# Nine groups instead of eight, and a row selection that spans all 128 rows

## The reference

```
x = x + 0.5 * fp4_ffn(layernorm(x))          # feed-forward, operands rounded to FP4 in blocks of 16
x = x + mamba(layernorm(x))                  # two layers, 256 channels, state of 16
x = x + 0.5 * fp4_ffn(layernorm(x))          # same weights as the first
x = x + 0.5 * experts(layernorm(x))          # 8 experts 128 -> 512 -> 128, gated by a thresholded sigmoid
x = x + attention(layernorm(layernorm(x)))   # 16 heads of 8, causal, relative bias
x = x + 0.5 * experts(layernorm(x))          # same weights as before
```

```
h_n[t] = exp(delta[t] * A_n) * h_n[t-1] + delta[t] * u[t] * B_n[t]
y[t]   = sum over n of h_n[t] * C_n[t]
```

## Time and profile before

| | |
|---|---|
| median of the runs shown | 2872.73 us |
| profiled execution, its own time | 2876.84 us |
| its span, first to last instruction | 2875.1 us |
| mean granted TensorE clock | 0.953 |
| instructions | 41563 |
| VectorE busy | 1946.4 us (68%) |
| ScalarE busy | 1606.0 us (56%) |
| GpSimd busy | 1371.3 us (48%) |

### The profile page before, as it was taken

One profiled execution on the slowest core, in us unless ns is written; L12 is line 12 of the kernel. 1 busy time (PEld: TensorE's weight loads), 2 busy tenths in 40 slices (PEclk: granted clock), 3 DMA queues, 4 the chain that ended last, 5 costly groups with the idle time before them and its releaser, 6 DMA issues.

```text
span 2875.1 us, 41563 instructions
## 1 busy us (share of the span) xinstructions
PE 2733.4 (95%) x14913; PEld 1895.2 (66%) x14913; DVE 1946.4 (68%) x3753; ACT 1606.0 (56%) x3405; POOL 1371.3 (48%) x1226
## 2 busy tenths in 40 slices
PE   7999999999999989999799899999999999999888
PEld 7777875786577655666366566656575666678675
DVE  5868887697868687676867886687858666432320
ACT  2433436435664556656486556756675676465654
POOL 2448475563737365454716474274636635311111
PEclk9999999999999989799799999999999999999899
DMA  4223122131213021211202121121202112000000
GB/s 147 67 67 104 55 64 74 45 92 42 79 40 96 23 73 39 70 49 49 77 20 78 37 76 31 49 70 31 75 19 86 36 52 67 1 4 1 1 5 4
DMA packets 88573, 150.60 MB, mean 52 GB/s; under 512 B 10565, under 2 KB 21485, under 8 KB 88110
## 3 DMA queue, kind: packets, MB, share of 16 engines
q1 hardware_dynamic: 88366, 147.94, 16.4%
HBM read 145.26 MB, written 2.65 MB: 51 GB/s over the span
## 4 chain that ended last, share of the span: by engine, by line
PE 83%; ACT 7%; DVE 5%; POOL 3%; issue 2%; DMA 0%; POOLq 0%; SPq 0%; ACTq 0%; DVEq 0%
PE c_bank L912 16%; PE c_bank L920 16%; PE c_bank L1338 13%; PE a_bank L758 8%; PE a_bank L748 5%; PE b_bank L1072 3%; PE b_bank L1061 3%; PE a_bank L727 2%; PE b_bank L1085 2%; PE b_bank L1084 2%; PE b_bank L582 1%; PE b_bank L563 1%; PE b_bank L565 1%; PE b_bank L1083 1%; PE a_bank L764 1%
## 5 line engine op out<-in xcount | busy, mean ns | idle before, releaser
L829 POOL TENSOR_TENSOR prod_c<-hst,prod_c 128x512 f32<-128x512 f32 x512 | 666.0, 1306 | 502.0 <-DVE hst L706 478.1
L706 DVE TENSOR_TENSOR_SCAN hst<-dA,a_bank 128x512 f32<-128x512 f32 x512 | 621.0, 1213 | 16.3 <-ACT dA L818 6.8
L912 PE MATMUL c_bank<-c_xT,w 128*128 128x512 f32 x1024 | 544.3, 638 | 7.7 <-ACT weighted_y L955 4.7
L818 ACT ACTIVATE dA<-delta,a_neg 128x510 f32<-128x510 f32 x512 | 364.2, 718 | 330.8 <-DVE hst L706 325.4
L920 PEld LDWEIGHTS c_bank<-w,hid 128*128 128x128 f32 x4096 | 491.2, 193 | 80.0 <-issue 47.5
L920 PE MATMUL c_bank<-w,hid 128*128 128x128 f32 x4096 | 529.4, 281 | 3.1 <-ACT hid L947 3.1
L1338 PEld LDWEIGHTS c_bank<-ident 128*128 128x128 f32 x3752 | 449.1, 193 | 66.4 <-issue 60.4
L1338 PE MATMUL c_bank<-ident 128*128 128x128 f32 x3752 | 483.4, 281 | 0.5 <-ACT weighted_y L955 0.4
L947 ACT ACTIVATE hid<-c_bank,b 128x512 f32<-128x512 f32 x512 | 349.7, 687 | 185.2 <-PE c_bank L912 183.5
L700 DVE TENSOR_TENSOR a_bank<-du,a_bank 128x512 f32<-128x512 f32 x512 | 350.5, 685 | 132.7 <-PE a_bank L748 128.5
L971 POOL TENSOR_TENSOR xs<-xs,weighted_y 128x512 f32<-128x512 f32 x128 | 167.9, 1312 | 544.6 <-ACT weighted_y L955 544.0
(11 more groups left out here) (179 smaller groups left out, 3550.8 us busy)
## 6 DMA issues: line engine op xcount, KB each, us to landing
prod_c<-c_rows SPq DMA_DIRECT2D x512, 256.0 KB, 3.1
w<-in_w SPq DMA_DIRECT2D x2, 2048.0 KB
xs<-in_x SPq DMA_DIRECT2D x8, 256.0 KB, 8.6
bias<-skew SPq DMA_DIRECT2D x1, 2048.0 KB, 8.8
out_dram<-xs SPq DMA_DIRECT2D x8, 256.0 KB, 2.3
in_wT<-in_in_wT SPq DMA_DIRECT2D x1, 512.0 KB
c_rows<-bcC SPq DMA_DIRECT2D x16, 32.0 KB, 1.6
b_hq<-in_w_gu SPq DMA_DIRECT2D x1, 384.0 KB, 3.2
```

Source lines behind the costliest of these rows:

```text
L706: nc.vector.tensor_tensor_scan(hst[:, s % RS, :], dA[:, s % RA, :], b_bank, 0.0, ALU.mult, ALU.add).then_inc(M.h.sem, 1)
L818: nc.scalar.activation(half_batches(dA[:, s % RA, :], 1), half_batches(delta[:, h, :], 1), ACT.Exp, scale=a_neg[:, l, h, n:n + 1]).then_in ...
L829: nc.gpsimd.tensor_tensor(prod[:, s % RP, :], hst[:, s % RS, :], cring[:, s % RC, :], ALU.mult).then_inc(M.pp.sem, 1)
L912: nc.tensor.matmul(S.bank[up_bank(e, c)][:, :], w1[:, e, c * 128:(c + 1) * 128], S.xT[:, :], start=True, stop=True).then_inc(M.up.sem, 1)
```

## The change

It has three parts. First, the groups are no longer of one size: `BATCHES = [1] + [2] * 7 + [1]`, nine groups, the first and the last with one batch (256 tokens, 2 tiles), the seven between with two. Every loop over tiles, every slice of tokens and every count of a semaphore takes its size from the group. Second, the selection spans all 128 rows. Third, the five order strings are new; `ORDER_PE` now holds 194 fillers.

```diff
-GB = 2
+BATCHES = [1] + [2] * 7 + [1]
+GB = max(BATCHES)
 TOK = GB * SEQ
 TT = TOK // 128
-GROUPS = BATCH // GB
+GROUPS = len(BATCHES)
+FIRST = [sum(BATCHES[:g]) * SEQ for g in range(GROUPS)]
...
         def x_of(g):
-            return xs[:, g % XR, :, :]
+            return xs[:, g % XR, 0:2 * BATCHES[g], :]
...
-        def mamba_pe(pe, L, S, M, l):
+        def mamba_pe(pe, L, S, M, l, g):
+            gb, tt, tok = BATCHES[g], 2 * BATCHES[g], SEQ * BATCHES[g]
...
-                    nc.tensor.matmul(S.bank[2 - s % 2 * 2][:, :], sel[64:128, s % NST, :], bc3[64:128, :],
+                    nc.tensor.matmul(S.bank[2 - s % 2 * 2][:, 0:tok], sel[:, s % NST, :], bc3[:, 0:tok],
                                      start=True, stop=True).then_inc(M.b.sem, 1)
...
+            if l == 0 and L.g == 0:
+                dve.wait_ge(s_const, 3 + RA)
...
-                        nc.tensor.matmul(S.bank[up_bank(e, c)][:, :], w1[:, e, c * 128:(c + 1) * 128], S.xT[:, :],
+                        nc.tensor.matmul(S.bank[up_bank(e, c)][:, 0:tok], w1[:, e, c * 128:(c + 1) * 128], S.xT[:, 0:tok],
                                          start=True, stop=True).then_inc(M.up.sem, 1)
...
-                    for t in range(TT):
+                    for t in range(tt):
                         for j in range(HC):
...
             pool.wait_ge(v_ones, 1)
-            pool.wait_ge(s_const, 1 + RA)
+            nc.gpsimd.memset(bc3[:, :], 0.0).then_inc(s_const, 1)
+            pool.wait_ge(s_const, 2 + RA)
             pool.wait_ge(s_wm, 16 * len(load_m))
-            nc.gpsimd.tensor_copy(sel[64:128, :, :], eye2[64:128, :].unsqueeze(2).to_broadcast([64, NST, 128])).then_inc(s_const, 1)
+            nc.gpsimd.tensor_copy(sel[:, :, :], eye2[:, :].unsqueeze(2).to_broadcast([128, NST, 128])).then_inc(s_const, 1)
```

More of the change, by code:

```diff
@@ L143, in __init__, with count, before @@
     def __init__(self, sem, per, use=0, uses=1):
-        self.sem, self.per = sem, per
-        self.before, self.total = use * per, uses * per
+        self.sem, self.per, self.use, self.uses = sem, per, use, uses
+    def count(self, g):
+        return self.per[g] if isinstance(self.per, list) else self.per
+    def before(self, g):
+        if isinstance(self.per, list):
+            return sum(self.per[:g])
+        return (self.uses * g + self.use) * self.per
 class Lane:
@@ L158, in at @@
     def at(self, signal, k):
-        assert 1 <= k <= signal.per
-        return signal.total * self.g + signal.before + k
+        assert 1 <= k <= signal.count(self.g)
+        return signal.before(self.g) + k
 def build(nc, a, out):
@@ L311, in __init__ @@
                 self.ev = sig(n + "_evacuated", 1, use, uses)
+        moe_order = [(0, 0)]
+        b_order = [(0, 0), (0, 1), (1, 0), (0, 2)]
+        for g in range(1, GROUPS):
+            moe_order += [(0, g), (1, g - 1)]
+            b_order += [(1, g), (0, g + 2), (2, g - 1)]
+        moe_order.append((1, GROUPS - 1))
+        b_order = [o for o in b_order if o[1] < GROUPS] + [(2, GROUPS - 1)]
+        ffn_order = [o for o in b_order if o[0] < 2]
+        ffn_tiles = [2 * BATCHES[g] for part, g in ffn_order]
+        ffn_pairs = [BATCHES[g] for part, g in ffn_order]
+        ffn_quants = [1 + BATCHES[g] for part, g in ffn_order]
+        att_heads = [BATCHES[g] * HEADS for g in range(GROUPS)]
         class FfnS:
@@ L1009, in y_end @@
                 yield
-            for r in range(NH):
+            for r in range(nh):
                 h = r % HEADS
@@ L1043, in attn_pe @@
                     pe.wait_ge(M.kH.sem, L.at(M.kH, g))
-                nc.tensor.matmul(S.bank[1][:, :], wkT[:, g, :], S.xT[:, :], start=True, stop=True).then_inc(M.k.sem, 1)
+                nc.tensor.matmul(S.bank[1][:, 0:tok], wkT[:, g, :], S.xT[:, 0:tok], start=True, stop=True).then_inc(M.k.sem, 1)
                 yield
-            for t in range(TT):
+            for t in range(tt):
                 ins = nc.tensor.matmul(S.bank[2][:, t * 128:(t + 1) * 128], S.xT[:, t * 128:(t + 1) * 128], wvT[:, :],
@@ L1050, in attn_pe @@
             yield
-            for r in range(NH + 4):
-                if r < NH:
+            for r in range(nh + 4):
+                if r < nh:
                     b, h = r // HEADS, r % HEADS
@@ L1155, in a_dve @@
                 for l in range(LAYERS):
[L1156 removed]
+                    yield from mamba_dve(dve, L, sa, mam[l], l, g)
         def a_pe(pe, L):
```

565 lines of the change are left out of this document (286 added, 279 removed).

## The result

The changed kernel takes 2837.63 us (median of four runs, 2836.68 to 2838.16), the kernel before in the same session 2874.28 us. The ratio is 0.986, 95% interval 0.984 to 0.989: 37 us or 1.3% faster. 2750 was forecast, and 2838 lies above the range (2665 to 2822). The profiled span is 2835.9 us, so the forecast span of 2754 is missed by 82 us. The mean granted clock fell from 0.953 to 0.881.

A forecast was written before the change was run, and what follows sets the result against it. TensorE bounds the loaded layers and end, lane a's pace on VectorE/GpSimd the light layers. 55 + 140 + 483 + 1860 + 286 = 2824 us, less 60 (selection) and 10 (fillers): 2754 span, said as 2750; range 2705 to 2795, eight in ten 2665 to 2822.

The forecast's parts named there:

- start, layers 1 and 2: Layer 1 begins at 55 us; layers 1 and 2, with 256 tokens at 0.6 of the old step, take 140 us.
- loaded layers with the old selection, fillers taken off: Layers 6 and 8 to 18: 1446 us of TensorE work times the old ratio 1.286 is 1860, less 10 for fillers.
- selection in the loaded layers: 384 lone selections each lose 0.19 us of entry and exit, 73 us; four fifths counted, 60 us saved.
- selection worth nothing: Rival: the selection's cost sits in type or queueing, so the 128-row edit saves nothing; 2812 us, chance 0.10.
- The first L937: Sign: the first expert up matmul (L912 in the old kernel) comes in layer 3, before 260 us.
- I take 10: Removing 575 filler instructions from loaded layers and end saves 10 us, between 0 and 64, any clock loss included.
- The argument against the clock: Behind the old last layer the clock was 0.94 with 42 filler instructions in 414 us, so fillers and clock go poorly together.
- I give them the old light times: Light two-batch layers 3, 4, 5 and 7 take 125, 105, 125 and 128 us, 483 in all.
- 1.216 behind the last layer: Behind the last layer, 235 us of TensorE work times the old kernel's ratio 1.216 there gives 286 us.
- The clock rival: Rival: without fillers from layer 4 on the granted clock falls and eats the gain; 2900 us at 0.90, chance 0.06.
- break-even of 0.91: Clock rival's threshold: 514 of 2875 us at half clock, mean clock 0.91; from there on slower than before.
- Groups worth nothing: Rival: small instructions' fixed cost or lane c's idling cancels the groups' gain, leaving only selection and fillers; 2803 us, chance 0.13.

The follow-up runs named there:

- Full-row scores: Changed kernel with score matmuls over all 128 rows instead of a head's 24 (scores sum four heads, not the reference's attention): 2754.75 us, 0.955 of the kernel before.
- wide products: Changed kernel with 96 columns instead of 9 moved through each attention product with v, result unchanged: 2801.27 us, 0.971 of the kernel before.

## Why the prediction was wrong

The sum taken apart by its own terms, with the trace of the changed kernel and that of the same kernel with the old selection:

| term | forecast | measured | difference |
|---|---|---|---|
| start, layers 1 and 2 | 195 | 196.5 | +1.5 |
| light layers 3, 4, 5, 7 | 483 | 531.1 | +48 |
| loaded layers with the old selection, fillers taken off (1860 - 10) | 1850 | 1906.8 | +57 |
| selection in the loaded layers | -60 | -120.3 | -60 |
| behind the last layer | 286 | 321.8 | +36 |

By the parts of the change, one after the other and by medians, it reads: selection -94 us (2876 to 2782; 60 were forecast), fillers out +68 (to 2850; -10 forecast), groups, order and 194 fillers -12 (to 2838; -51 forecast). The three errors are -34, +78 and +39 us and make the miss as well. In another order of the steps the shares differ, since with the old selection the fillers are worth 56 us and not 68.

**Right.** What a selection costs at entry and exit and that both parts of it go, by the spacings above. The small layers: 83 and 60 us, with a step of VectorE of 1.10 us. The rival "selection worth nothing" falls. The first L937 is in layer 3, but at 274 us, not before 260. The Trainium skill ("TensorE: Matmul & The Clock Gate", section "Why this matters for your kernels") gives K=32 the time of K=128; with other matmuls between, a selection over 64 rows and one over 128 measure 0.19 us apart each time. "TensorEngine Tiling (Array Packing)" of the Trainium skill (section "Tiling Modes") says that a change of mode drains TensorE; the trace agrees, with a cost at the entry and one at the exit.

**Right by luck: the loaded layers.** 1786.5 us against 1790 is the sum of two errors, +57 and -60. Four fifths of 0.19 us were counted for each of 384 selections, and 0.31 was measured, beside 121 us less of half clock. In the old kernel it was 73 us for 352, or 0.21 each. In the six light layers of the changed kernel the selection gave 11 us in all, so there "hidden behind the scan" nearly holds. The 33 us in the light layers of the old kernel are a property of its fillers.

**Failed: "I take 10" for the fillers, with the clock inside it.** This is the step with the largest price. The fillers were priced by their streaming, as 10 us of gain. In the old kernel the last 216, in the loaded layers and behind them, were worth 23 and 21 us instead, and all of them 56 and 68. In the changed kernel with the old selection the loaded layers have 393 us of half clock, against 214 in those of the old kernel (whose work is 5% less), and are 57 us over the forecast; what part of the 57 is fillers and what part the new order was not separated. The argument against the clock was 0.94 behind the last layer with 42 fillers, one place.

**Failed: "I give them the old light times".** First a slip: 125, 125 and 128 stand where the earlier trace rows say 131.2, 130.9 and 132.4, 16 us. It did no harm, by luck: with the new selection the old layers 3, 5 and 7 take 124.1, 124.1 and 125.7 us, 373.9 in all. Against these the changed kernel's 428.0 are 54 us more. VectorE's busy time in the three is 110.8 + 120.4 + 123.7 = 355 us against 325, so 30 us are work that was moved in, and its idle time grew by 24. VectorE was not added up by layer in the forecast; the table of steps had only TensorE's. Of the 24 us, 14 lie behind the last recursion of a layer, where VectorE mostly waits for TensorE, and 8 between the first and the last. VectorE's longest waits in layer 3 of the changed kernel:

```profile
DVE xc L705 <- PE a_bank L778: 5.9, 1, 5.9
DVE xc L648 <- ACT xc L799: 5.2, 2, 3.8
DVE b_quant_scales L497 <- ACT b_xn L476: 5.2, 1, 5.2
DVE hm L734 <- PE a_bank L784: 2.5, 1, 2.5
```

The columns are total us, times, longest. The selection's own wait is down to 0.8 us. The first and the last of these waits fall in the layer's last 11 us, in which the clock was 1.00 and expert matmuls stood ahead of lane a's. How much of the 24 us the half clock has elsewhere was not separated; that another order would shorten these waits was not tried.

**Failed: 1.216 behind the last layer.** It was 321.8/235 = 1.37. The forecast's mix of work is nearly the old one (81 of 235 us are lane b's, 107 of 341 before). What differs in the traces is that the first heads stand closer together and that half clock there went from 46 us in 414 to 89 in 322. Full-row scores bring the factor to 1.22 and wide products to 1.27, so few rows and few columns are the cause, in the main by the half clock that goes with them.

**The rivals.** None happened as written. The clock rival had the mechanism, but its break-even of 0.91 was wrong: the mean was 0.881, and the kernel was still faster. It took half of every microsecond at half clock as lost; of 672 such us, 317 lie before the end of layer 7, where TensorE has room. And the selection paid for part of the rest. "Groups worth nothing" has nearly the right size for groups (12 us at most, fillers included) by the wrong mechanism: the small instructions cost what was forecast, and layers 1 and 2 took 143 us. The gain of the small groups is visible but spent: when twelve batch-layers are done (12 times one batch through one layer) the changed kernel stands at 852.8 us (end of layer 7) and the old one with the new selection at 787.2 (end of layer 6), and from there both need the same, 1983 and 1981 us. So the shorter end is paid for by then.

**What stays open.** Groups and strings were not separated, since a string fits only its groups. That the end reacts to rows and columns is shown; why the chip grants half clock to a TensorE that is never idle is not.

## What to carry to other kernels

Of a change in several parts, run each alone: here one line was worth 94 us, and the rest took 56 of them back. Before removing matmuls that nobody reads, read where TensorE has room (there they cost little and may hold the clock) and where the clock falls without them; their streaming time is not their price. When work moves into a stage, add it up on every engine of that stage, not only on the one that bounds the whole.

## What the runs showed of the hardware

- A matmul over 64 of the 128 rows between full-row ones costs 0.095 us going in and 0.100 coming out. The same instruction over all rows, the unused ones zero, costs nothing more. For the two score matmuls of a head over 24 rows it is some 0.22 us together.
- TensorE can show busy for 64.8 of 64.8 us and be granted half clock all the while. Moving 96 instead of nine columns in the same instructions raised the clock behind the last layer from 0.86 to 0.94 and shortened the kernel by 36 us.
- Half clock cost little where TensorE had room: the old layer 3 with the new selection took 127.7 us at 0.64, without fillers, and 124.1 at 1.00, with them, and its layer 2 lost 8 us to 71 of half clock; the changed kernel's layer 4 103.1 at 0.64 and 102.9 at 0.97.
- Six fillers ahead of each of 57 steps made a layer of 256 tokens 49 us longer.
